# Moving mask work, conversions and two PSUM banks in the attention stage of a cross-attention and mixture kernel

## The reference

```python
qp = layernorm(x) @ Wq.T                      # 16 heads of 32
k, v = split(ctx @ Wkv_expand.T)              # ctx has width 128; only its first 512 rows matter
scores = einsum('bhqd,bhkd->bhqk', qh, kh) / sqrt(32)
scores = where(causal, scores, lowest)        # query i sees keys 0..i
x = x + (softmax(scores) @ vh) @ Wout.T
logits = layernorm(x) @ router_w.T + router_b # per token 512 x 8
c = top-2 weights per (token, output), summed to (token, expert)
x = x + sum_e c[:, e] * (layernorm(x) @ expert_w[e].T + expert_b[e])
```

## Time and profile before

| | |
|---|---|
| median of three executions | 2067.4 us |
| the profiled execution's own time | 2067.4 us |
| its span, first to last instruction | 2065.6 us |
| PE busy | 1986.0 us (96%) |
| DVE busy | 1451.6 us (70%) |
| ACT busy | 1046.7 us (51%) |
| POOL busy | 854.5 us (41%) |
| mean granted PE clock | 0.987 |

### The profile page before, as it was taken

How to read it: one execution, slowest core, us unless ns; L and a number is a source line. 1 busy time by engine, 2 the same in 40 slices (tenths; PEclk the granted TensorE clock), 3 DMA queues, 4 the chain that set the end, 5 groups by cost and what they waited for, 6 DMA issues and landing times.

```text
span 2065.6 us, 31279 instructions
## 1 busy us (share of the span) xinstructions
PE 1986.0 (96%) x9994; PEld 1532.4 (74%) x10044; DVE 1451.6 (70%) x3010; ACT 1046.7 (51%) x2093; POOL 854.5 (41%) x987
## 2 busy tenths in 40 slices
PE   5899999999987999999999999999999999999999
PEld 3667677676754777777777777778888888888887
DVE  5677767766656577777777777478787788787532
ACT  2666566556534367767677677544333344333300
POOL 3687777777666235344353543212111132111100
PEclk8999999999998999999999999999999999999999
DMA  5455454554453545454554544553222223222110
GB/s 158 119 129 136 125 140 126 136 148 119 124 185 123 205 154 183 162 208 163 192 181 152 206 175 187 201 186 112 87 76 87 86 89 110 87 76 85 52 41 31
DMA packets 99218, 275.84 MB, mean 134 GB/s; under 512 B 13435, under 2 KB 14480, under 8 KB 95030
## 3 DMA queue, kind: packets, MB, share of 16 engines
q1 hardware_dynamic: 94518, 216.16, 33.0%
q10 hardware_dynamic: 4608, 58.72, 8.3%
HBM read 131.67 MB, written 92.27 MB: 108 GB/s over the span
## 4 chain that ended last, share of the span: by engine, by line
PE 86%; DVE 5%; DMA 2%; POOL 2%; issue 2%; ACT 1%; SPq 1%; ACTq 0%; DVEq 0%; POOLq 0%
PE pair L265 21%; PE pair L267 21%; PE pair L266 21%; PE pair L636 3%; PE pair L669 3%; PE ps L682 3%; PE ps L265 3%; PE ps L266 3%; PE ps L267 3%; PE pair L880 2%; DVE pair L1312 1%; SPq L371 1%; PE ps L702 1%; DVE nmax L1306 1%; ACT pT L1044 1%
## 5 line engine op out<-in xcount | busy, mean ns | idle before, releaser
L265 PE MATMUL pair<-w_h,hT 128*128 128x512 f32 x1920 | 797.1, 415 | 3.5 <-DVE xb L1644 1.9
L267 PE MATMUL pair<-w_h,hT 128*128 128x512 f32 x1920 | 751.7, 392 | 0.0
L266 PE MATMUL pair<-w_l,hT 128*128 128x512 f32 x1920 | 747.6, 389 | 0.0
L1837 POOL TENSOR_TENSOR logits<-logits,second 128x512 f32<-128x512 f32 x224 | 298.3, 1367 | 609.1 <-DVE second L1523 608.8
L267 PEld LDWEIGHTS pair<-w_h,hT 128*128 128x128 f32 x1920 | 360.6, 188 | 80.2
L266 PEld LDWEIGHTS pair<-w_l,hT 128*128 128x128 f32 x1920 | 361.6, 188 | 74.7
L265 PEld LDWEIGHTS pair<-w_h,hT 128*128 128x128 f32 x1920 | 363.3, 189 | 71.4 <-issue 2.3
L1644 DVE SCALAR_TENSOR_TENSOR xb<-pair,c_now,xb 128x512 f32<-128x512 f32 x256 | 191.9, 750 | 190.4 <-PE pair L267 183.2
L1044 ACT ACTIVATE pT<-pair,zero 128x1024 f32<-128x1024 f32 (+3 forms) x256 | 202.5, 792 | 203.1 <-PE pair L669 200.2
L1312 DVE CUSTOM_DVE_ANT_0 pair<-pair,future 128x256 f32<-128x256 f32 (+3 forms) x340 | 184.3, 554 | 128.7 <-PE pair L636 121.1
L636 PE MATMUL pair<-qk_st 96*128 96x256 f32 (+3 forms) x512 | 160.9, 344 | 22.0 <-DVE nmax L1312 11.4
(11 more groups left out here) (171 smaller groups left out, 2847.8 us busy)
## 6 DMA issues: line engine op xcount, KB each, us to landing
logits<-lg_all ACTq DMA_DIRECT2D x32, 1792.0 KB, 7.9
qk_st<-qk SPq DMA_DIRECT2D x384, 128.0 KB, 2.3
lg_all<-ev_a SPq DMA_DIRECT2D x32, 768.0 KB, 6.4
lg_all<-ev_b SPq DMA_DIRECT2D x32, 768.0 KB, 3.3
xb<-x SPq DMA_DIRECT2D x64, 256.0 KB, 3.0
hT_all<-hT SPq DMA_DIRECT2D x32, 512.0 KB, 3.6
hT<-hT_all SPq DMA_DIRECT2D x32, 512.0 KB, 3.8
xt<-in_x SPq DMA_DIRECT2D x8, 1024.0 KB, 5.4
```

The costliest lines, as they stand in the source:

```text
L265: pe.matmul(dst, lh, rh, start=start, stop=False)
L266: pe.matmul(dst, lh, rl, start=False, stop=False)
L267: return pe.matmul(dst, ll, rh, start=False, stop=stop)
L1837: pool.tensor_tensor(logits[t % 2][:, e - 1, :], logits[t % 2][:, e - 1, :], second[:], ALU.subtract)\
```

## The change

`masked(c, v)` becomes true for all 8 units of group 0, and in the other groups for all target units `vv` of 4 and more, which are `v` of 1 to 4 where it was 3 and 4. New among the masked are so `v` = 0, 1, 2 of group 0 and `v` = 1, 2 of groups 1 to 3. `STATISTICS` moves from (2,0), (2,1), (3,0), (3,1) to (2,1), (3,0), (3,1), (3,2). `NORMALISED` moves from (2,7), (3,1), (3,3), (3,7) to (3,1), (3,5), (3,6), (3,7). `SPLIT` moves groups 0 and 1 one unit earlier, and group 2 from unit (0,1) of the next batch to (3,6), except in the last batch, where it stays in the epilogue. The two banks of the transposes are exchanged.

```diff
--- before.py
+++ after.py
@@ -273,7 +273,7 @@
 
         def masked(c, v):
 
-            return v in (3, 4) or c == 0 and v > 4
+            return c == 0 or target(c, v)[1] >= QB
 
         def block_of(v):
 
@@ -284,15 +284,16 @@
         QUERY = {0: 0, 2: 1, 3: 2, 4: 3}
         VALUE = {0: 0, 2: 1, 3: 2, 4: 3}
         SUMMED = 1
-        STATISTICS = ((2, 0), (2, 1), (3, 0), (3, 1))
-        NORMALISED = ((2, 7), (3, 1), (3, 3), (3, 7))
+        STATISTICS = ((2, 1), (3, 0), (3, 1), (3, 2))
+        NORMALISED = ((3, 1), (3, 5), (3, 6), (3, 7))
         LAST_GROUP = {3: 0, 5: 1, 7: 2}
         TURNED = {6: (0, 1), 7: (2, 3)}
         OUT_BUF = (0, 1, 2, 0)
         INVERTED = 2
         REFINED = 3
         SCALED = 4
-        SPLIT = {(3, 5): 0, (3, 6): 1, (0, 1): -2, (0, 6): -1}
+        SPLIT_LATE = (3, 6)
+        SPLIT = {(0, 6): -1, (3, 4): 0, (3, 5): 1, (3, 6): 2}
         ADDS = 2 * (QB - 1)
 
         def key_bank(c):
@@ -780,8 +781,8 @@
                         project_out(b - 1, i, chunk, 0)
 
                     def turn_tokens(i):
-                        take(1 - i % 2, "LNT", (b + 1) * QB + i)
-                        norm_turn((b + 1) * QB + i, i, 1 - i % 2)
+                        take(i % 2, "LNT", (b + 1) * QB + i)
+                        norm_turn((b + 1) * QB + i, i, i % 2)
 
                     for v in range(UNITS):
                         out = not first and out_block(c, v, last) is not None
@@ -1054,12 +1055,12 @@
                             hi_of(n + AHEAD, QH, "q", 1)
                         if c == 0 and more:
                             for i in TURNED.get(v, ()):
-                                turned_tokens((b + 1) * QB + i, i, 1 - i % 2)
+                                turned_tokens((b + 1) * QB + i, i, i % 2)
                         if v == key_step(c) and ahead:
                             hi_of(n + AHEAD, KH, "k", key_bank(c))
                         if v == TURN and (more or c < KC - 1):
                             hi_shift(n + 1)
-                        if (c, v) in SPLIT and not (first and c == 0):
+                        if (c, v) in SPLIT and not (first and c == 0) and not (last and (c, v) == SPLIT_LATE):
                             d = SPLIT[c, v]
                             hi_outputs(n - c + d, d % KC, b if d >= 0 else b - 1)
                         if v == INVERTED and not (first and c == 0):
@@ -1779,7 +1780,7 @@
                             split_context(b + 1)
                         if not more and (c, v) in SELECTED:
                             select_bias(SELECTED.index((c, v)))
-                        if (c, v) in SPLIT and not (first and c == 0):
+                        if (c, v) in SPLIT and not (first and c == 0) and (more or (c, v) != SPLIT_LATE):
                             d = SPLIT[c, v]
                             lo_outputs(n - c + d, d % KC)
                         if (c, v) in STATISTICS and further:
```

## The result

The changed kernel takes 2088.98 us in the median of 4 executions (2087.92 to 2092.16), against 2067.53 (2066.21 to 2068.1): a ratio of 1.0107, with a 95% interval of 1.009 to 1.0125. That is 21.5 us slower.

The account below looks back on a forecast made before the run. It took attention to be bound by PE's instruction stream. Batches 1 to 5 at 11.8 us, batch 0 at 3.2, batch 6 at 0.8 and the last at 0.5 made 16.3 us on 2067.4, so 2083.7 us; range 2070 to 2089.

Parts of the forecast that it names:

- The end of a batch: Group 3: 2.64 us more POOL work against 0.83 of slack makes PE's L702 2.1 us later, covering ACT's delay.
- The banks: Start of group 1: the projection waits for block 2 alone, gaining 0.6 us in each of batches 1 to 6.
- What DVE gains: Masked units: DVE saves about 0.3 us each, but the result comes no earlier, so the saving gets no value.
- The masks: Newly masked units, 9 in a batch: each costs PE 0.19 us; 13 us for all 70 if none were hidden.
- The sum: Attention: 11.8 us for batches 1 to 5, 3.2 batch 0, 0.8 batch 6, 0.5 the last; 16.3 us slower.
- 1: Rival at the batch end: the tables are hidden, only masks and banks remain, about 6 us, 2073; chance 0.14.
- 2: Rival at PE's waits for DVE, units 5 and 6: DVE's queue was the wait, faster, 2062; chance 0.10.
- 4: Rival at unit 7 and after: ACT's and POOL's delays add up, 3.4 us a batch and more, 2090; chance 0.04.
- 3: Rival across attention: waits absorb most masks and the banks pay for the rest, 2067 within 4; chance 0.10.

Follow-up runs that it names:

- masks_only: The kernel before with the new masked() alone, tables and banks as before: 2080.27 us, 1.0067.
- masks_g0: The kernel before with all of group 0 masked (units 0, 1, 2 new), nothing else: 2074.03 us in a single execution.
- norm_back: The changed kernel with NORMALISED put back to its places before: 2085.48 us, 1.0097 to the kernel before.
- after_p2: The changed kernel without an edit, in a further profiled execution: 2085.63 us.
- masks_banks: The changed kernel with STATISTICS, NORMALISED and SPLIT put back, so masks and banks only: 2076.46 us, 1.0042 to the kernel before.
- after: The changed kernel without an edit, in its first profiled execution: 2085.55 us.
- stats_back: The changed kernel with STATISTICS put back: 2084.82 us, 1.0086 to the kernel before.
- stats_only: The kernel before with the new STATISTICS alone: 2072.75 us in a single, profiled execution.
- split_only: The kernel before with the new SPLIT and its condition alone: 2069.75 us in a single, profiled execution.
- tables_only: The kernel before with the new STATISTICS, NORMALISED and SPLIT alone: 2079.51 us, 1.0058.
- split_back: The changed kernel with SPLIT put back: 2085.03 us, 1.0095 to the kernel before.
- norm_only: The kernel before with the new NORMALISED alone: 2071.03 us in a single, profiled execution.

## Why the prediction was wrong

The direction, the place and the mechanism of a middle batch held; the size of the whole did not. 16.3 us were forecast and 21.5 measured. The time lies at the very edge of the range (2088.98 against 2089; as a ratio 1.0107 against 1.0105), and that edge was not earned: 2.6 us instead of 2.1 at each of six batch ends gives 2087, not 2089. Step by step:

- **The end of a batch** (2.1 us, decided by POOL, with ACT's 1.2 beside it): right. The tables alone cost 1.8 = 2.64 - 0.83 a batch, putting NORMALISED back changes no middle batch, and putting STATISTICS or SPLIT back frees PE of POOL and leaves it to ACT.
- **The banks** (-0.6): right, -0.6 a batch.
- **What DVE gains** (nothing): right. The reduction took 0.693 us, and PE's waits for maxima stayed at 0.30 to 0.40 us.
- **The masks** (0.19 each): the price is right in group 0 and a little low in groups 1 and 3 (0.21 to 0.22, masks_only), and the cover in group 0 was not there: I let a wait hide half a unit, and masks_g0 shows all three paid. A batch costs 2.45 us and not 2.35, and batches 1 to 5 together 12.4 in norm_back against 11.8.
- **The sum** is where it failed. It was made of stretches at a clock of 1.00 and has no term for the clock, which it put at nothing without a reason, although the prediction itself forecast new waits of PE. In the changed kernel's profile attention ends 19.7 us later and not 16.3: batch 0 with its end costs 4.3 (forecast 3.2), batches 1 to 5 13.1 (11.8), batch 6 1.1 (0.8) and the last 1.2 (0.5). 1.4 us of the difference are two falls of the clock, at the ends of batches 0 and 1: each of these ends takes 0.7 us more than in norm_back, where PE waits 0.55 us instead of 1.24 for ACT at the first and not at all at the second, and after_p2 shows the first end without a fall and without the 0.7. 0.5 us are the masks. The other 1.5 lie in the start of the program, batch 6 and the last batch, where executions of this one kernel differ by as much (attention ends 19.3 to 21.0 us later in its five profiles), and are not explained.
- **One execution for all of them.** The sum took the profiled execution for the timed ones, as was true of the kernel before. The profiled execution after is 18.2 us longer and not 19.7, since it has no fall of the clock at the passage to the experts and the one before has: its expert stage is 1.7 us shorter, 1.6 of them by the clock. With such a fall it would have taken some 2087.2 us, an estimate from 2085.55 and these 1.6. That is half of the 3.4 us between it and the median of the timed ones; the other half is open. So the forecast of the profiled execution, 1.9 us off, was closer than its parts deserve.
- **Rivals.** Of 1, only the masks' part is true (masks_banks, +0.4%). 2, that DVE's queue was the wait, and 4, that the delays add up, are refuted by masks_only and norm_back, though the time that 4 named, 2090, is nearer to the measured one than mine. 3 falls with the time.

The Trainium skill's figure for warm matmuls of 128 columns, 56 ns from start to start (page "TensorE: Matmul & The Clock Gate", section "Wait — 56ns, not 53.3ns?"), is not what these mask matmuls take. Two of them, each with a weight load of its own, take 0.18 us from the first to the instruction behind them (342.13 to 342.31), so 0.09 each.

The best kernel measured is the kernel before with only the banks exchanged, 2062.10 us, 0.22% faster (0.12 to 0.32). The rest of the change costs about 1.3%.

## What to carry to other kernels

When an engine's instructions are moved, look for the longest run without a gap on that engine and how far ahead of its reader it ends: here 0.83 us decided, and of 2.64 us of "idle engine" work only that much was free. Of two delays that end at the same instruction only the longer counts, so undoing the shorter one shows nothing. And a waiting tensor engine can cost more than its wait: add to a forecast what the clock may take. Before you compare two profiled executions, compare the stages that the change doesn't touch: here one of them differed by 1.7 us, 1.6 of them by the clock.

## What was not expected of the hardware

The granted clock fell behind waits of PE of 0.60 and 1.24 us that ended 2.2 us apart (after), and not behind 0.51 and 1.24 us at the same place (after_p2). In stats_back it fell behind waits of 0.72 us in some batches and not in others with the same instructions (74.3 against 75.95 us). At the passage to the experts it fell behind a wait of 1.87 us (before) and not behind one of 2.94 (after). In the profiles in which only POOL holds PE up at the middle batch ends (norm_back, stats_only, split_only) it fell at none of the ends of batches 0 to 5; where ACT does, it fell at one to three of them.

Where PE waits for POOL a little later in the batch, a fall made a middle batch 0.4 to 0.8 us longer (the changed kernel, tables_only); where it doesn't, 1.5 to 1.6 us (stats_back, split_back, norm_only). That the wait takes up the rest is my reading: in the changed kernel's batch with the fall the wait for POOL is gone.
